# Norm chains, weight pieces, row parts and semaphore clears in a two-layer transformer kernel on one core

## The reference

```
x = x + 0.5 * moe(norm(x))        # 8 experts, top 2 by router, 2 shared experts
x = x + attention0(norm(x))       # 16 heads of 8, causal over 1024 positions
x = x + 0.5 * moe(norm(x))        # the same weights again
x = x + 0.5 * fp4_ffn(norm(x))    # activations and weights in blocks of 16, FP4 values
x = x + attention1(norm(x))       # 16 heads of 64, 4 by 4 scores over the leading axis
x = x + 0.5 * fp4_ffn(norm(x))    # the same weights again
```

## Time and profile before

| what | value |
| --- | --- |
| median of three executions | 2107.71 us (2106.75 to 2108.11) |
| the profiled execution | 2103.85 us |
| its span, first to last instruction | 2102.1 us |
| TensorE matmul busy | 1707.6 us, 81% |
| VectorE busy | 1345.0 us, 64% |
| ScalarE busy | 876.7 us, 42% |
| GpSimd busy | 620.4 us, 30% |
| mean granted TensorE clock | 0.928 |

### The profile page before, as it was taken

The page is one execution under the profiler, slowest core; times in us unless marked ns, Lnnn a source line. Parts: engine busy times, 40 slices in busy tenths (PEclk is TensorE's granted clock), DMA queues, the critical chain, the costliest instruction groups (busy, mean ns, idle before and its releaser), DMA issues. The chain is left out here.

```text
span 2102.1 us, 31391 instructions
## 1 busy us (share of the span) xinstructions
PE 1707.6 (81%) x10505; PEld 1173.3 (56%) x10505; DVE 1345.0 (64%) x2565; ACT 876.7 (42%) x1530; POOL 620.4 (30%) x669
## 2 busy tenths in 40 slices
PE   3987783999999999999399788257579999999475
PEld 2656661544544444443276676135347888888254
DVE  5534356877777777774463344579887666663796
ACT  2323331466666666667132333123224444444232
POOL 2355453211111011111226654213213333334132
PEclk9989996999999999999679898679879999999798
DMA  6022321111011111110402132100100000000000
...
DMA packets 47705, 82.35 MB, mean 39 GB/s; under 512 B 10948, under 2 KB 32900, under 8 KB 46532
## 3 DMA queue, kind: packets, MB, share of 16 engines
...
...
## 5 line engine op out<-in xcount | busy, mean ns | idle before, releaser
L1824 DVE TENSOR_REDUCE z_parts<-z_pM 128x4 f32<-128x512 f32 x576 | 380.3, 687 | 144.6 <-PE z_pM L1576 78.3
L1745 ACT ACTIVATE z_Pr<-z_pE 128x512 f32<-128x512 f32 x576 | 326.4, 599 | 198.6 <-PE z_pE L1600 190.1
L1600 PE MATMUL z_pE<-z_QM,z_QK 128*128 128x512 f32 x576 | 265.1, 465 | 0.9 <-ACT z_Pr L1745 0.9
L1576 PE MATMUL z_pM<-z_KM,z_Q 128*128 128x512 f32 x576 | 247.7, 432 | 14.1 <-DVE z_parts L1824 7.6
L1928 POOL TENSOR_SCALAR_AFFINE_SELECT z_Pr<-z_Pr 128x512 f32<-128x512 f32 x128 | 81.5, 637 | 541.2 <-ACT z_Pr L1745 540.3
L1389 POOL TENSOR_TENSOR a_pm<-a_Pn,k_mask 128x512 f32<-128x512 f32 x128 | 132.4, 1059 | 271.4 <-PE a_pT L1227 153.4
L456 POOL DMA_INDIRECT slot_results<-m_yq,m_xq x156 | 150.8, 967 | 129.1 <-ACT m_yq L639 97.8
L1600 PEld LDWEIGHTS z_pE<-z_QM,z_QK 128*128 128x128 f32 x576 | 108.8, 190 | 134.3 <-ACT z_Pr L1745 103.0
L421 POOL DMA_INDIRECT slot_rows<-m_XN,m_dest x128 | 124.2, 970 | 162.7 <-issue 64.7
L1613 PE MATMUL z_pO<-z_Pr,z_V 128*9 128x512 f32 (+3 forms) x1536 | 159.7, 488 | 0.4 <-POOL z_Pr L1928 0.3
L1576 PEld LDWEIGHTS z_pM<-z_KM,z_Q 128*128 128x128 f32 x576 | 108.3, 188 | 80.5 <-DVE z_parts L1824 71.6
...
## 6 DMA issues: line engine op xcount, KB each, us to landing
...
z_QM<-z_Q SPq DMA_DIRECT2D x128, 64.0 KB, 2.0
z_KM<-z_QK SPq DMA_DIRECT2D x60, 128.0 KB, 2.4
m_raw<-in_gu SPq DMA_DIRECT2D x2, 2048.0 KB, 8.9
...
```

What stands on the lines that cost most here:

```text
L1576: last = mm(pM[n % 2][:, :].rearrange("p (h k) -> p h k", h=4), Q[G % 2][:, qt * P:(qt + 1) * P], KM[G % 2][:, :, kb * P:(kb + 1) * P], st ...
L1600: mm(pE[e % 3][:, :].rearrange("p (h c) -> p h c", h=4), QK[G % RING][:, kt * P:(kt + 1) * P], QM[half][:, :, q * P:(q + 1) * P], start=Tr ...
L1745: a.activation(Pr[j % 4][:, :, q * P:(q + 1) * P], pE[e % 3][:, :].rearrange("p (h c) -> p h c", h=4), ACT.Exp, scale=DH0 ** -0.5).then_in ...
L1824: v.tensor_reduce(parts[:, qt, kb, :], pM[n % 2][:, :].rearrange("p (h k) -> p h k", h=4), AX.X, ALU.max).then_inc(maxed, 1)
```

## The change

Six things are changed. Names and line numbers of the changed kernel differ by up to some 60 lines from those before.

1. Semaphores of a scope are set back by four engines, a quarter each.
2. In the mixture stages ScalarE loads its square root table and makes the square root first; `wh` of the shared experts is rounded after row group 3, `wh` of the routed experts in four pieces after steps 9 to 12 of the shared phase, and `wl` is made by VectorE in five pieces (after row group 5 and after steps 15, 17, 19 and 21). TensorE waits for five pieces ahead of the experts.
3. In attention0 the square root comes first, `wh` after row group 1, `wl` on VectorE after group 2. GpSimd clears half a key tile at the start, ScalarE the other half; everything else that GpSimd clears, and its bias addition, comes after the last normalisation. 14 busy products instead of 24, and no wait ahead of them.
4. In the entry of attention1 ScalarE's square root comes ahead of the weight rounding; GpSimd makes `wl` in the next scope in ten pieces and then adds the bias to X; TensorE waits piece by piece, and VectorE no longer adds the bias.
5. x is loaded in four parts, and its statistics are taken in the loading scope, part by part.
6. The last stage stores X pair by pair as each is updated; the scope o is gone.

The diff:

```diff
@@ -32,10 +32,26 @@
-                    for sem in self.sems:
+                    for sem in self.sems[0::4]:
...
+                @block.vector
+                def _(dve):
+                    for sem in self.sems[1::4]:
+                        dve.sem_clear(sem)
+                @block.scalar
+                def _(act):
+                    for sem in self.sems[2::4]:
+                        act.sem_clear(sem)
+                @block.sync
+                def _(sp):
+                    for sem in self.sems[3::4]:
+                        sp.sem_clear(sem)
@@ -198,9 +215,10 @@
-                load.scalar(act)
+                nc.scalar.activation(warm_table[:, :], ident[:, 0:1], ACT.Sqrt)
...
+                load.scalar(act)
@@ -351,6 +369,11 @@
+        warm_table = s.sb("warm_table", [P, 1])
+        PIECES, HIGH_AT, LOW_AT = 4, (9, 10, 11, 12), (15, 17, 19, 21)
+        piece = lambda i: slice(i * E_ROUTED * GU // PIECES, (i + 1) * E_ROUTED * GU // PIECES)
+        sgu_loaded = s.sem("sgu_loaded")
@@ -380,7 +403,7 @@
-                sp.dma_start(raw[:, nr:], d["sgu"]).then_inc(gu_loaded, 16)
+                sp.dma_start(raw[:, nr:], d["sgu"]).then_inc(sgu_loaded, 16)
@@ -420,9 +443,6 @@
-                for part, (a, z) in enumerate(((E_ROUTED * GU, E_ALL * GU), (0, E_ROUTED * GU))):
-                    pool.wait_ge(w_high, part + 1)
-                    g_.tensor_tensor(wl[:, a:z], raw[:, a:z], wh[:, a:z].bitcast(F32), ALU.subtract).then_inc(w_low, 1)
@@ -541,7 +561,7 @@
-                        pe.wait_ge(w_low, 2)
+                        pe.wait_ge(w_low, 1 + PIECES)
@@ -591,9 +611,7 @@
-                for part, (lo, z) in enumerate(((E_ROUTED * GU, E_ALL * GU), (0, E_ROUTED * GU))):
-                    act.wait_ge(gu_loaded, 32)
-                    a.activation(wh[:, lo:z], raw[:, lo:z], ACT.Copy).then_inc(w_high, 1)
+                a.activation(warm_table[:, :], ident[:, 0:1], ACT.Sqrt)
@@ -602,6 +620,10 @@
+                    if w == 3:
+                        act.wait_ge(sgu_loaded, 16)
+                        c = slice(E_ROUTED * GU, E_ALL * GU)
+                        a.activation(wh[:, c], raw[:, c], ACT.Copy).then_inc(w_high, 1)
@@ -609,6 +631,10 @@
+                    if n in HIGH_AT:
+                        act.wait_ge(gu_loaded, 16)
+                        c = piece(HIGH_AT.index(n))
+                        a.activation(wh[:, c], raw[:, c], ACT.Copy).then_inc(w_high, 1)
@@ -654,7 +680,7 @@
-                emit_norm_statistics(nc, C, dve, std_ready, var_ready, step, 0, mv, std, rstd, tmp, measured=(turn > 0))
+                emit_norm_statistics(nc, C, dve, std_ready, var_ready, step, 0, mv, std, rstd, tmp, measured=True)
@@ -676,6 +702,10 @@
+                def low_weights(c, k):
+                    dve.wait_ge(w_high, k)
+                    v.tensor_tensor(wl[:, c], raw[:, c], wh[:, c].bitcast(F32), ALU.subtract).then_inc(w_low, 1)
@@ -683,6 +713,8 @@
+                    if w == 5:
+                        low_weights(slice(E_ROUTED * GU, E_ALL * GU), 1)
@@ -758,6 +790,8 @@
+                    if n in LOW_AT:
+                        low_weights(piece(LOW_AT.index(n)), 2 + LOW_AT.index(n))
@@ -936,7 +970,18 @@
+        stored = s.sem("stored")
...
+            @block.sync
+            def _(sp):
+                if out is not None:
+                    for k in range(NP2):
+                        c = slice(k * TP2 * D, (k + 1) * TP2 * D)
+                        sp.wait_ge(x_updated, k + 1)
+                        sp.dma_start(out[:, c], X[:, c]).then_inc(stored, 16)
+                    sp.wait_ge(stored, 16 * NP2)
@@ -1109,9 +1154,10 @@
+        self.raw = s.sb("raw", [P, 3 * INNER1])
...
-        self.raw, self.bv, self.bvw = t.sb("raw", [P, 3 * INNER1]), t.sb("bv", [P, CH1]), t.sb("bvw", [P, CH1, P])
+        self.bv, self.bvw = t.sb("bv", [P, CH1]), t.sb("bvw", [P, CH1, P])
@@ -1131,8 +1177,6 @@
-        pool.wait_ge(self.high_done, 1)
-        self.nc.gpsimd.tensor_tensor(self.wl[:, :], self.raw[:, :], self.wh[:, :].bitcast(F32), ALU.subtract)
@@ -1214,6 +1258,8 @@
+                        if isinstance(w, int) and w == 0:
+                            pe.wait_ge(wl_ready, r + 1)
@@ -1231,6 +1277,8 @@
+                        if isinstance(w, int) and w == 1:
+                            pe.wait_ge(wl_ready, CH1 + 2)
@@ -1271,7 +1319,6 @@
-                pe.wait_ge(zeroed, 2)
@@ -1335,6 +1382,8 @@
+                        if isinstance(w, int) and w == 1:
+                            dve.wait_ge(bias_added, 1)
@@ -1363,11 +1412,7 @@
-                xs = X[:, :].rearrange("p (t f) -> p t f", f=D)
-                v.tensor_tensor(xs, xs, Wt["bo"][:, :].unsqueeze(1).to_broadcast([P, NT, D]), ALU.add).then_inc(bias_added, 1)
...
-                dve.wait_ge(bias_added, 1)
@@ -1390,6 +1435,15 @@
+                pieces = lambda t, r: t[:, 0:2 * INNER1].rearrange("p (k c) -> p k c", k=2)[:, :, r * P:(r + 1) * P]
+                for r in range(CH1):
+                    g.tensor_tensor(pieces(Wt["wl"], r), pieces(Wt["raw"], r), pieces(Wt["wh"], r).bitcast(F32), ALU.subtract).then_inc(wl_ready, 1)
+                for u in range(2):
+                    c = slice(2 * INNER1 + u * 512, 2 * INNER1 + (u + 1) * 512)
+                    g.tensor_tensor(Wt["wl"][:, c], Wt["raw"][:, c], Wt["wh"][:, c].bitcast(F32), ALU.subtract).then_inc(wl_ready, 1)
+                xs = X[:, :].rearrange("p (t f) -> p t f", f=D)
+                g.tensor_tensor(xs, xs, Wt["bo"][:, :].unsqueeze(1).to_broadcast([P, NT, D]), ALU.add).then_inc(bias_added, 1)
@@ -1664,13 +1721,12 @@
-                pe.wait_ge(ready, 3)
-                keep_busy(nc, C, pM[1][:, :], 24)
-                pe.wait_ge(w_low, 1)
+                keep_busy(nc, C, pM[1][:, :], 14)
...
+                        pe.wait_ge(w_low, 1)
@@ -1686,6 +1742,7 @@
+                        pe.wait_ge(ready, 3)
@@ -1771,14 +1828,16 @@
-                act.wait_ge(loaded, 16)
-                a.activation(wh[:, :], raw, ACT.Copy).then_inc(w_high, 1)
...
-                act.wait_ge(ready, 3)
+                a.activation(KM[0][:, 2:4, :], ident[:, 0:1].unsqueeze(2).to_broadcast([P, 2, SEQ0]), ACT.Copy, scale=0.0).then_inc(km_zeroed, 1)
...
+                    if w == 1:
+                        act.wait_ge(loaded, 16)
+                        a.activation(wh[:, :], raw, ACT.Copy).then_inc(w_high, 1)
@@ -1870,7 +1929,6 @@
-                dve.wait_ge(ready, 3)
@@ -1890,9 +1948,13 @@
+                    if w == 2:
+                        dve.wait_ge(w_high, 1)
+                        v.tensor_tensor(wl[:, :], raw, wh[:, :].bitcast(F32), ALU.subtract).then_inc(w_low, 1)
...
+                dve.wait_ge(ready, 3)
@@ -1927,13 +1989,13 @@
-                g_.memset(KM[0][:, :, :].bitcast(F32), 0.0).then_inc(zeroed, 1)
+                g_.memset(KM[0][:, 0:2, :].bitcast(F32), 0.0).then_inc(zeroed, 1)
+                pool.wait_ge(xn_ready, NT)
+                g_.memset(parts[:, :, :, :], -BIG).then_inc(ready, 1)
...
-                g_.memset(parts[:, :, :, :], -BIG).then_inc(ready, 1)
...
-                pool.wait_ge(w_high, 1)
-                g_.tensor_tensor(wl[:, :], raw, wh[:, :].bitcast(F32), ALU.subtract).then_inc(w_low, 1)
-                for buf in (KM[1], QM[0], QM[1]):
+                for buf in (QM[0], KM[1], QM[1]):
@@ -1962,10 +2024,15 @@
+            XPARTS = 4
+            x_loaded = [t.sem(f"x_loaded{u}") for u in range(XPARTS)]
...
-                    for dst, src in ((X[:, :], "x"), (C["ident"][:, :], "c_ident"), (C["rank"][:, :], "c_rank"),
+                    for part in range(XPARTS):
+                        c = slice(part * NT * D // XPARTS, (part + 1) * NT * D // XPARTS)
+                        sp.dma_start(X[:, c], d["x"][:, c]).then_inc(x_loaded[part], 16)
+                    for dst, src in ((C["ident"][:, :], "c_ident"), (C["rank"][:, :], "c_rank"),
@@ -1973,7 +2040,11 @@
-                    dve.wait_ge(loaded, 8 * 16)
+                    for part in range(XPARTS):
+                        dve.wait_ge(x_loaded[part], 16)
+                        for k in range(part * NT // XPARTS, (part + 1) * NT // XPARTS):
+                            measure(nc, C, k)
+                    dve.wait_ge(loaded, 7 * 16)
@@ -1992,14 +2063,7 @@
-            fp4_stage(nc, C, "f2", fp4)
-        with Scope(nc, "o") as t:
-            stored = t.sem("stored")
-            with nc.Block() as block:
-                @block.sync
-                def _(sp):
-                    sp.dma_start(out, X[:, :]).then_inc(stored, 16)
-                    sp.wait_ge(stored, 16)
+            fp4_stage(nc, C, "f2", fp4, out)
```

16 lines of the change are left out of this document (10 added, 6 removed).

## The result

The changed kernel takes 2042.05 us (median of 4 runs, 2038.67 to 2045.17) where the kernel before takes 2107.44 on the same chip (2106.75 to 2108.11): a ratio of 0.9689, 95% interval 0.9668 to 0.9711. Its profiled execution took 2038.97 us with a span of 2037.1, so 65.0 us less span than before, where the prediction's sum was 66.5. The forecast was 2041.2 us, its range 2036 to 2046. The granted clock was 0.938 on average, 0.928 before.

A forecast was written before the change was run, and what follows sets the result against it. The prediction saw norm chains waiting for unneeded work, scope-end gaps growing with semaphores, and a late last store. Its gains, less 1.0 us for the shared phases, sum to 66.5 us: 2107.7 to 2041.2 us, range 2036 to 2046.

The forecast's parts named there:

- A: Start and m1: statistics in the loading scope and a 4.0 us norm chain bring first rows near 16.0 us; gain 19.9.
- B: m2: the norm chain from aggregation to first rows falls from 24.36 to 4.0 us; gain 20.4.
- The cost in the shared phases: Weight pieces on ScalarE and VectorE in m1 and m2: between 0 and 8.0 us a stage, taken as 0.5 each.
- C: Attention0: 11.4 us from the shorter chain, less 1.4 for moved weights and 4.7 for a stalled copy; gain 5.3.
- D: Entry of attention1: chain loses its 4.9 us stall, but TensorE must first finish 16 bias matmuls; gain 4.0 us.
- E: First slots of attention1: `wl` in pieces releases TensorE earlier, first key operation comes sooner; gain 2.5 us (0 to 4.4).
- F: Scope ends: sharing semaphore clears leaves 160 fewer in line at 0.064 us each; gain 10.2 us (0 to 10.2).
- G: End of the kernel: storing pair by pair leaves a last part of 128 KB; gain 5.2 us (4.5 to 5.6).
- no stall: Rival, 15%: attention0's copy of the first maximum slips in between two GpSimd operations; 2036.5 us.
- the clears were dearer: Rival, 10%: semaphore clears on other engines cost some four times as much, so sharing them gains 0; 2051.4 us.
- the key clears were not held up: Opposed rival, 6%: in attention1 GpSimd's whole stream keeps out VectorE's two key clears, 14.3 us more; 2055.5 us.
- The slower case: Rival, 1%: pieces leave TensorE gaps, its clock stays low in both turns' shared phases, 88 us more; 2129 us.

The follow-up runs named there:

- old-chain experiment: Changed kernel with ScalarE's old rounding order back in m1, and in m2 also GpSimd's two long subtractions; 2073.63 us, one run.
- changed kernel's second trace: The changed kernel run once more without any edit, on another chip; 2041.95 us (5 runs), ratio 0.9689 to the kernel before.

## Why the prediction was right, point by point

- **A and B** held to 0.1 us: both chains come down to the 4.0 us of the earlier trace rows. The old-chain experiment gives the shares: in m1 12.7 us for ScalarE's order, and the other 35.95 - 28.89 = 7.1 for GpSimd's operation, whose stall in m2 was 7.04 instead of 0.19. The parts of x are worth 3.8 us, but not on top of these: they lie within the 12.7, since with the old order the rounding ends the wait.
- **The cost in the shared phases,** 0.5 us a stage, was right or still too high: 0.3 us more in m1 and none in m2. The bound of 8 us a stage was far off: even doubled pieces show no cost.
- **C failed in size.** The step "I take 4.7" for the copy on top of the bias addition had the mechanism, the place and the length right (4.70 us) but priced only VectorE. TensorE was idle for 4.44 us in it and ran at 1.2 GHz until some 15 us behind it, which cost 5.7 us more. The prediction gave the low clock a price for the busy products at the start of this stage (at most 1.6) and, as a rival, in the shared phase, but none behind the stall. With it C is 5.3 - 5.7 = -0.4, and 0.1 was measured.
- **D** was right because it asked what is late next: TensorE's bias matmuls. **E** came out 0.3 us better than taken.
- **F was mis-sized:** 8.5 us instead of 10.2. The fixed part and GpSimd's price were right, but the sum took 0.064 us for every engine and VectorE's clear costs 0.087. With that price for VectorE's share the gaps would sum to 10.4 instead of 9.2 us; 10.9 was measured. Of the missing 0.5, 0.35 lies behind attention0, and its cause stays open.
- **G** came out 0.4 us better.
- **The sum came out better than its terms.** C and F together missed by 6.9 us. From first rows to last statistics, m1 and m2 gave 1.6 and 2.6 us where 0.5 each was to be lost, 5.2 us the other way. In the changed kernel's second trace the same two stretches took 2.1 us more each than before the change, so this is luck and no effect of the change that I could show. Of the rivals, none took place: no stall would have needed another GpSimd order, the clears were dearer but on one engine and by a third, the key clears were not held up, x in four parts came sooner than in one, and the pieces cost next to nothing. The slower case, a clock that stays low, has its small picture in attention0.
